# Two expert mixtures whose activations stay in PSUM, rounded by ScalarE and completed by VectorE

## The reference

```python
# mixture one (_L1_ffn_ref): E=8 experts, 128 -> 512 -> 128
h1 = jnp.einsum('bth,efh->btef', x, w1) + b1
h1 = jax.nn.gelu(h1, approximate=False)
expert_outputs = jnp.einsum('btef,ehf->bteh', h1, w2) + b2
# the top 2 of the router's logits, softmax over them, weighted sum
...
# mixture two (_L2_ffn_ref): E=8 experts, 128 -> 2 x 256 -> 128
gu = jnp.einsum('th,eih->tei', x, w13_weight)
gate, up = (gu[..., :INTER], gu[..., INTER:])
act = jax.nn.silu(gate) * up
act = act * combine[:, :, None]
out = jnp.einsum('tei,ehi->th', act, w2_weight)
```

## Time and profile before

| | |
|---|---|
| time, median of three runs | 500.97 us (497.62 to 504.19) |
| span of the profiled execution, first to last instruction | 496.1 us |
| its own time beside the span | not recorded; the median of the runs is 4.9 us above the span |
| PE busy | 412.7 us, 83% |
| DVE busy | 363.1 us, 73% |
| ACT busy | 201.8 us, 41% |
| POOL busy | 197.1 us, 40% |
| mean granted TensorE clock | 0.875 |

### The profile page before, as it was taken

The page is one execution under the profiler, slowest core; times in us unless marked ns, Lnnn a source line. Parts: engine busy times, 40 slices in busy tenths (PEclk is TensorE's granted clock), DMA queues, the critical chain, the costliest instruction groups (busy, mean ns, idle before and its releaser), DMA issues.

```text
span 496.1 us, 5961 instructions
## 1 busy us (share of the span) xinstructions
PE 412.7 (83%) x1982; PEld 315.9 (64%) x1982; DVE 363.1 (73%) x690; ACT 201.8 (41%) x351; POOL 197.1 (40%) x162
## 2 busy tenths in 40 slices
PE   1747888868799999999699997499999986899965
PEld 0526664866566666676379996366666644799834
DVE  4211858577569999998777748959999997777256
ACT  1100131325377666654174531234444321645245
POOL 4100106312568988885110006236576634000052
PEclk9999795675899999999599996679999985999757
DMA  8300000010110011110001000011111000000001
GB/s 272 150 0 0 2 0 1 1 44 0 46 46 18 25 44 42 32 32 2 0 0 33 1 2 0 0 38 32 32 33 32 1 1 0 1 1 0 2 0 42
DMA packets 8638, 12.52 MB, mean 25 GB/s; under 512 B 1131, under 2 KB 4757, under 8 KB 8613
## 3 DMA queue, kind: packets, MB, share of 16 engines
q1 hardware_dynamic: 7984, 11.58, 7.2%
q0 software_dynamic: 96, 0.32, 0.3%
q10 hardware_dynamic: 533, 0.31, 0.2%
HBM read 11.54 MB, written 0.52 MB: 24 GB/s over the span
## 4 chain that ended last, share of the span: by engine, by line
PE 40%; DVE 30%; issue 15%; ACT 7%; POOL 4%; DMA 2%; SPq 0%; DVEq 0%; ACTq 0%; POOLq 0%
DVE rhi L1065 7%; PE bank L1544 6%; PE bank L1208 3%; PE bank L1526 3%; PE bank L1209 3%; PE bank L1210 3%; DVE shared L1154 3%; DVE rhi L1157 2%; DVE wa L1044 2%; DMA mats<-in_mats 2%; ACT shared L776 2%; PE bank L1216 2%; PE bank L1432 2%; PE bank L1435 1%; POOL rstd L363 1%
## 5 line engine op out<-in xcount | busy, mean ns | idle before, releaser
L363 POOL TENSOR_TENSOR rstd<-var,neghalf 128x4 f32<-128x4 f32 x16 | 16.3, 1018 | 156.5 <-DVE var L809 156.5
L432 POOL TENSOR_TENSOR rlo<-shared,rhi 128x512 fp32r<-128x512 f32 x40 | 56.3, 1408 | 45.3 <-DVE rhi L1157 22.7
L1208 PE MATMUL bank<-hhi,wuh 128*128 128x512 f32 x128 | 53.6, 419 | 9.6 <-issue 4.9
L1065 DVE CAST rhi<-shared 128x512 fp32r<-128x512 f32 x48 | 53.4, 1114 | 7.3 <-ACT shared L675 7.3
L675 ACT ACTIVATE shared<-bank,b1s 128x512 f32<-128x512 f32 x64 | 43.9, 687 | 27.3 <-PE bank L1210 25.7
L1209 PE MATMUL bank<-hlo,wuh 128*128 128x512 f32 x128 | 53.1, 415 | 0.0
L1210 PE MATMUL bank<-hhi,wul 128*128 128x512 f32 x128 | 52.7, 411 | 0.0
L1432 PE MATMUL bank<-rhi,wdh 128*128 128x512 f32 x96 | 41.5, 432 | 10.7 <-POOL rlo L432 8.7
L442 POOL TENSOR_TENSOR wb<-wb,wa 128x512 f32<-128x512 f32 x28 | 41.0, 1463 | 14.8 <-DVE wa L1044 14.8
L1124 DVE TENSOR_REDUCE small<-bank 128x6 f32<-128x462 f32 (+1 forms) x48 | 27.8, 579 | 19.2 <-PE bank L1210 19.2
L1071 DVE TENSOR_TENSOR rlo<-shared,rhi 128x512 fp32r<-128x512 f32 x32 | 37.7, 1178 | 5.2 <-ACT rhi L679 4.7
(11 more groups left out here) (272 smaller groups left out, 924.3 us busy)
## 6 DMA issues: line engine op xcount, KB each, us to landing
up_raw<-in_w SPq DMA_DIRECT2D x8, 258.0 KB, 2.7
down_raw<-in_w SPq DMA_DIRECT2D x8, 256.0 KB, 2.9
up_raw<-in_v SPq DMA_DIRECT2D x8, 256.0 KB, 2.7
down_raw<-in_v SPq DMA_DIRECT2D x8, 128.0 KB, 2.7
const<-in_const SPq DMA_DIRECT2D x1, 913.0 KB, 11.7
mats<-in_mats SPq DMA_DIRECT2D x1, 640.0 KB, 10.2
mats<-in_mats SPq DMA_DIRECT2D x1, 576.0 KB, 9.0
x<-in_x SPq DMA_DIRECT2D x2, 256.0 KB, 3.5
```

The source lines that it names most:

```text
L432: nc.gpsimd.tensor_tensor(rlo[n % 4][:, :], ring[n % 4][:, :], rhi[n % 4][:, :].bitcast(F32), ALU.subtract).then_inc(lo, 1)
L1065: V.tensor_copy(rhi[n % 4][:, :], ring[n % 4][:, :]).then_inc(q["hiD"], 1)
L1208: mm(o, lh, rh, start=start, stop=False)
```

## The change

Mixture one: Gelu writes its result into the bank from which it reads. The rounding reads that bank and is done by ScalarE for chunks 0, 2 and 3 of each four, one chunk late (`high1(n-1)` behind Gelu n), and by VectorE for chunk 1. All rests are VectorE's, from the bank. A bank may be overwritten when the rest of its chunk is done, no longer when the Gelu is.

Mixture two: Silu still writes `ring`, but `mul` writes its product into the gate bank. All roundings are ScalarE's (`high2(n-1)` behind Silu n), all rests VectorE's (`low2(n-1)` behind `mul` n). Hidden n makes the up half first, which waits for `mul` n-2, then the gate half, which waits for the rest of chunk n-2.

GpSimd's `low` and its calls go (L432; those hunks and the renamed semaphores are left out below, and so are unchanged lines around the edits).

```diff
@@ -277,11 +277,8 @@
-        LO_POOL1 = {n for n in range(N1) if n % 4 in (0, 2)}
-        HI_ACT1 = {n for n in range(N1) if n % 4 == 1}
-        LO_POOL2 = {1, 5}
-        ALL1, ALL2 = set(range(N1)), set(range(N2))
-        HI_DVE1, LO_DVE1, LO_DVE2 = ALL1 - HI_ACT1, ALL1 - LO_POOL1, ALL2 - LO_POOL2
+        HI_DVE1 = {n for n in range(N1) if n % 4 == 1}
+        HI_ACT1 = set(range(N1)) - HI_DVE1
         BANKS1 = [1, 2, 3, 7]
@@ -489,8 +478,6 @@
                         split_down(i + 1, 0, C2, r)
-                    if n in LO_POOL2:
-                        low(n, r["hi"], N2 * i + n + 1, r["loP"])
                     if n % 2 == 1:
@@ -660,6 +647,13 @@
+            def high1(i, n):
+
+                if n % N1 not in HI_ACT1:
+                    return
+                act.wait_ge(q["gelu"], N1 * i + n + 1)
+                nc.scalar.activation(rhi[n % 4][:, :], bank[BANKS1[n % 4]][:, :], ACT.Copy).then_inc(q["hiA"], 1)
+
             def body1(i, last):
@@ -672,11 +666,10 @@
                     act.wait_ge(q["h"], g + 1)
-                    nc.scalar.activation(ring[n % 4][:, :], bank[BANKS1[n % 4]][:, :], ACT.Gelu,
+                    nc.scalar.activation(bank[BANKS1[n % 4]][:, :], bank[BANKS1[n % 4]][:, :], ACT.Gelu,
                                          bias=b1s[p][:, c:c + 1]).then_inc(q["gelu"], 1)
-                    if n in HI_ACT1:
-                        act.wait_ge(q["gelu"], g + 1)
-                        nc.scalar.activation(rhi[n % 4][:, :], ring[n % 4][:, :], ACT.Copy).then_inc(q["hiA"], 1)
+                    if n > 0 or not i_is(i, 0):
+                        high1(i, n - 1)
                     if i_is(i, 0) and n in (5, 6):
@@ -692,6 +685,7 @@
             body1(PASSES - 1, True)
+            high1(PASSES - 1, N1 - 1)
             output(PASSES - 1, G1 - 1, G1, C1, q["free"], q["add"], q["ys"])
@@ -732,6 +726,11 @@
+            def high2(i, n):
+
+                act.wait_ge(r["mul"], N2 * i + n + 1)
+                nc.scalar.activation(rhi[n % 4][:, :], bank[BANKG[n % 2]][:, :], ACT.Copy).then_inc(r["hi"], 1)
+
             def body2(i, last):
@@ -747,6 +746,8 @@
                     nc.scalar.activation(ring[n % 4][:, :], bank[BANKG[n % 2]][:, :], ACT.Silu).then_inc(r["silu"], 1)
+                    if n > 0 or not i_is(i, 0):
+                        high2(i, n - 1)
                     if n % 2 == 1:
@@ -754,6 +755,7 @@
             body2(PASSES - 1, True)
+            high2(PASSES - 1, N2 - 1)
             output(PASSES - 1, G2 - 1, G2, C2, r["free"], r["add"], r["ys"])
@@ -1060,16 +1062,14 @@
                     g = N1 * i + n
-                    if n not in HI_ACT1:
+                    if n in HI_DVE1:
                         dve.wait_ge(q["gelu"], g + 1)
-                        V.tensor_copy(rhi[n % 4][:, :], ring[n % 4][:, :]).then_inc(q["hiD"], 1)
-                    if n not in LO_POOL1:
-                        if n in HI_ACT1:
-                            dve.wait_ge(q["hiA"], len(HI_ACT1) * i + before(HI_ACT1, n + 1))
-                        else:
-                            dve.wait_ge(q["hiD"], len(HI_DVE1) * i + before(HI_DVE1, n + 1))
-                        V.tensor_tensor(rlo[n % 4][:, :], ring[n % 4][:, :], rhi[n % 4][:, :].bitcast(F32),
-                                        ALU.subtract).then_inc(q["loD"], 1)
+                        V.tensor_copy(rhi[n % 4][:, :], bank[BANKS1[n % 4]][:, :]).then_inc(q["hiD"], 1)
+                        dve.wait_ge(q["hiD"], len(HI_DVE1) * i + before(HI_DVE1, n + 1))
+                    else:
+                        dve.wait_ge(q["hiA"], len(HI_ACT1) * i + before(HI_ACT1, n + 1))
+                    V.tensor_tensor(rlo[n % 4][:, :], bank[BANKS1[n % 4]][:, :], rhi[n % 4][:, :].bitcast(F32),
+                                    ALU.subtract).then_inc(q["lo"], 1)
                     if n % 4 == 2:
@@ -1147,18 +1147,20 @@
+            def low2(i, n):
+
+                dve.wait_ge(r["hi"], N2 * i + n + 1)
+                V.tensor_tensor(rlo[n % 4][:, :], bank[BANKG[n % 2]][:, :], rhi[n % 4][:, :].bitcast(F32),
+                                ALU.subtract).then_inc(r["lo"], 1)
+
             def body2(i, last):
                 for n in range(N2):
                     g = N2 * i + n
                     dve.wait_ge(r["silu"], g + 1)
-                    V.tensor_tensor(ring[n % 4][:, :], ring[n % 4][:, :], bank[BANKU[n % 2]][:, :],
+                    V.tensor_tensor(bank[BANKG[n % 2]][:, :], ring[n % 4][:, :], bank[BANKU[n % 2]][:, :],
                                     ALU.mult).then_inc(r["mul"], 1)
-                    dve.wait_ge(r["mul"], g + 1)
-                    V.tensor_copy(rhi[n % 4][:, :], ring[n % 4][:, :]).then_inc(r["hi"], 1)
-                    if n not in LO_POOL2:
-                        dve.wait_ge(r["hi"], g + 1)
-                        V.tensor_tensor(rlo[n % 4][:, :], ring[n % 4][:, :], rhi[n % 4][:, :].bitcast(F32),
-                                        ALU.subtract).then_inc(r["loD"], 1)
+                    if n > 0 or not i_is(i, 0):
+                        low2(i, n - 1)
                     if n % 2 == 1:
@@ -1166,6 +1168,7 @@
             body2(PASSES - 1, True)
+            low2(PASSES - 1, N2 - 1)
             for j in range(G2 - B, G2):
@@ -1448,7 +1451,7 @@
                     pe.wait_ge(q["ul"], 2 * i + p + 1)
-                wait_positive(pe, q["gelu"], g - 3)
+                wait_positive(pe, q["lo"], g - 3)
                 w = slice(c * P, (c + 1) * P)
@@ -1467,10 +1470,7 @@
                                start=True, stop=True).then_inc(m["b2"], 1)
-                    if n in LO_POOL1:
-                        down(i, n, last, C1, G1, q, q["loP"], len(LO_POOL1) * i + before(LO_POOL1, n + 1))
-                    else:
-                        down(i, n, last, C1, G1, q, q["loD"], len(LO_DVE1) * i + before(LO_DVE1, n + 1))
+                    down(i, n, last, C1, G1, q, q["lo"], N1 * i + n + 1)
@@ -1489,7 +1489,7 @@
             body1(PASSES - 1, True)
-            pe.wait_ge(q["gelu"], N1 * PASSES)
+            pe.wait_ge(q["lo"], N1 * PASSES)
             finish(0, q, G1)
@@ -1595,8 +1595,10 @@
                 wait_positive(pe, r["mul"], g - 1)
-                for bk, off in ((BANKG[n % 2], 0), (BANKU[n % 2], F2)):
+                for bk, off in ((BANKU[n % 2], F2), (BANKG[n % 2], 0)):
                     w = slice(off + c * P, off + (c + 1) * P)
+                    if off == 0:
+                        wait_positive(pe, r["lo"], g - 1)
                     last = mm3(bank[bk][:, :], wuh[p][:, w], wul[p][:, w], hhi[b][:, :], hlo[b][:, :], True, True)
@@ -1608,10 +1610,7 @@
                         weights_T(1, n)
-                    if n in LO_POOL2:
-                        down(i, n, last, C2, G2, r, r["loP"], len(LO_POOL2) * i + before(LO_POOL2, n + 1))
-                    else:
-                        down(i, n, last, C2, G2, r, r["loD"], len(LO_DVE2) * i + before(LO_DVE2, n + 1))
+                    down(i, n, last, C2, G2, r, r["lo"], N2 * i + n + 1)
```

More of the change, by code:

```diff
@@ L240, in flamingo_program @@
         q = {n: sem(f"q_{n}") for n in
-             ["h", "gelu", "hiA", "hiD", "loD", "loP", "free", "uh", "ul", "dh", "dl", "ys", "row", "mult", "add"]}
+             ["h", "gelu", "hiA", "hiD", "lo", "free", "uh", "ul", "dh", "dl", "ys", "row", "mult", "add"]}
         r = {n: sem(f"r_{n}") for n in
-             ["g", "silu", "mul", "hi", "loD", "loP", "free", "uh", "ul", "dh", "dl", "ys", "row", "mult", "add"]}
+             ["g", "silu", "mul", "hi", "lo", "free", "uh", "ul", "dh", "dl", "ys", "row", "mult", "add"]}
         kv = {n: sem(f"kv_{n}") for n in ["pe", "act", "pool", "rep", "reps", "bd", "hi"]}
@@ L427, in _ @@
                 norm(k)
-            def low(n, hi, count, lo):
-                pool.wait_ge(hi, count)
-                nc.gpsimd.tensor_tensor(rlo[n % 4][:, :], ring[n % 4][:, :], rhi[n % 4][:, :].bitcast(F32),
-                                        ALU.subtract).then_inc(lo, 1)
             def add(i, j, groups, mult, done):
@@ L453, in body1 @@
                         split_down(i + 1, 0, C1, q)
-                    if n in LO_POOL1:
-                        low(n, q["hiD"], len(HI_DVE1) * i + before(HI_DVE1, n + 1), q["loP"])
                     if i_is(i, 0) and n == 11:
```

## The result

The changed kernel takes 506.45 us in the median (505.13 to 510.46, four runs) against 502.44 us before, a ratio of 1.0128 with an interval of 1.0074 to 1.0182. So it is slower by some 1.3%: the whole interval lies above 1, and the difference is under 2%. 505.9 us was forecast. Single executions can be over 1.5% slower than the fastest of the same kernel; the ratios leave these out, so a ratio can differ from the quotient of two medians.

A forecast was written before the change was run, and what follows sets the result against it. Mixture one was held by VectorE and GpSimd hindering each other, mixture two would be by a loop of handovers; 496.1 - 9.2 + 14.1 + 4.9 gave 505.9 us, range 498 to 518 us.

The forecast's parts named there:

- Mixture one, TensorE's floor: Four chunks in mixture one take 6.09 us on TensorE; ten waits of 0.74 us for GpSimd's rests go, 7.4 us.
- Its start: Mixture one's first down: ScalarE rounds chunk 0 during VectorE's routing, VectorE ends the rest at 125.3 us; 1.5 us off.
- Its end: Mixture one's last down, at 233.08 us, loses the 0.28 us idle before it; 0.3 us off.
- The cast from PSUM: VectorE's cast of chunk 1 of each four in mixture one, now reading PSUM, takes 0.6 us.
- The slack of 0.3 us: Chunk 3 before a weight copy in mixture one: rest ready after 3.6 us, needed after 3.9, so the wait stays hidden.
- Mixture two's loop: From one chunk's last gate matmul through Silu, product and rest to the next: 2.95 us a chunk against 2.56 before.
- rival three: Granted clock falls to 1.2 GHz in mixture two's idle gaps: 540 us if throughout, 523 us for half; chance 0.12.
- The drain: End of mixture two: 0.2 us shorter, the last rounding no longer queuing behind another Silu.
- The start of mixture two: Silu 2 and 3 stand behind weights on ScalarE; chunk 4's last matmul at 334.9 instead of 331.20 us, 3.7 us lost.
- Rival one: Not slower: mixture two's handovers overlap, its loop below 2.77 us a chunk; 495.5 to about 500 us; chance 0.13.
- rival two: Slower: mixture one's in-place Gelu takes 0.99 us or more, ScalarE's group 6.5 us; 6.4 us more, 512.3 us; chance 0.13.
- The sum: Whole kernel: span 496.1 - 9.2 + 14.1 = 501.0 us, plus 4.9 us between span and median: 505.9 us, 1% slower.

The follow-up runs named there:

- own_keys_splits_later: Changed kernel, mixture two's roundings and rests behind their own chunk, last attention's key products moved into it, GpSimd's first pass awaiting combine weights: 485.60 us, ratio 0.9707.
- two_only: Mixture two as changed, mixture one as in the kernel before: 517.79 us, ratio 1.0307 against the kernel before.
- two_low_own: Changed kernel, but in mixture two VectorE forms the rest of chunk n ahead of the product of n+1; ScalarE's lag stays: 508.83 us, ratio 1.0168.
- two_gate_first: Changed kernel with the halves of mixture two's hidden step in the old order, gate half first: 534.67 us, ratio 1.0621.
- one_ring: Changed kernel, but mixture one's Gelu writes to the SBUF buffer ring, where roundings and rests read it: 508.17 us, ratio 1.0123.

## Why the prediction was right

- **Mixture one, TensorE's floor.** 6.09 us a group were forecast as the new pace, 6.10 came. Ten waits of 0.74 us are gone, 7.4 us.
- **Its start** was forecast at 1.5 us and brought 0.7 (from chunk 3's last hidden matmul to the first down 4.23 us before, 3.56 after). The step that failed was that VectorE is free at 124.6 as before. This trace is 2.1 us ahead of the one before, so that would be 122.5; the first rest started at 123.31. GpSimd, without the rests ahead of it, reached its weights while VectorE was still at the routing, and a small instruction with two SBUF sources stood behind it:

```profile
121.56 1.26 POOL L392 TENSOR_TENSOR wdl<-down_raw,wdh 128x512 fp32r<-128x512 f32 x1 [2.67 <-ACT wdh L549]
...
121.91 1.00 DVE L1012 TENSOR_TENSOR rank<-rank,rinv 128x64 f32<-128x64 f32 x1
...
124.14 0.47 PE L1435 MATMUL bank<-rhi,wdh 128*128 128x512 f32 x1 [2.93 <-DVE rlo L1071]
```

  The same instruction took 0.22 us in the kernel before; own_keys_splits_later put this to the test. Its end brought nothing of the 0.3 us, since the last down still waits for its rest:

```profile
223.05 0.51 PE L1435 MATMUL bank<-rhi,wdh 128*128 128x512 f32 x1 [0.23 <-DVE rlo L1071]
```

  Together 7.9 us instead of 9.2.
- **The cast from PSUM** on VectorE was put at 0.6 us and took 0.681 in the median of 16. VectorE had room for it, so nothing came of it.
- **The slack of 0.3 us** at a group's last chunk held: no wait of TensorE for a rest from 136 to 220 us.
- **Mixture two's loop** was forecast at 2.95 us and measured 2.98; two_only, two_low_own and two_gate_first put its parts to the test (2.98, 2.88 for 2.86, 3.72 for 3.66). From chunk 4 to chunk 31 that makes 0.8 us. A further 0.6 us is one step of 3.59 us (326.31 to 329.90), in which the granted clock had gone to its 1.2 GHz level (0.57 from 326 to 330 us) after two waits of 1.1 and 1.9 us for the rests of chunks 1 and 2; rival three, for one chunk. The drain, from chunk 31's last hidden matmul to the last down, was to be 0.2 us shorter and isn't: 4.34 us before, 4.35 after.
- **The start of mixture two**: chunk 2 to chunk 4 took 10.42 us instead of 6.76, 3.7 us more, as forecast.
- **Rival one** fell, **rival two** too (the Gelu in place got shorter, below). **Rival three** showed for 3.6 us and never in the steady part, not even in two_gate_first from 355 to 435 us, where TensorE was busy 13.7 to 14.9 us of every 20; at the start of that kernel's mixture two it showed for 6 us.
- **The sum** was made with 4.9 us around the span, taken from the median. The changed kernel's profiled execution took 505.88 us with a span of 504.1, so 1.8 us lie around it; the rest was the distance of the profiled execution from the median. Span to span the forecast was +4.9 us, the traces say +8.0, of which 1.3 are the size of mixture one's gain, 1.6 that of mixture two's loss and 0.2 the unchanged stretches. The medians differ by 4.0 us (506.45 and 502.44), half of what the traces say; the four runs of the kernel before alone lie 6.6 us apart. The mechanism of both mixtures was right; that the time was hit to within 1 us is luck, since both mixtures came out slower than forecast by 2.9 us together.

## What to carry to other kernels

Moving work off busy engines pays only where they set the pace. Before a step is put one item later in a queue, look for a buffer that is held until it is done: here a lag of one chunk on two queues and two banks held until the end made a loop of 2.98 us out of work that TensorE does in 2.36, and the same edit without the lag is 2 to 3% faster than the kernel before. An assistant engine can cost more than it brings: taking GpSimd's 32 rests back to a VectorE that looked full (24.83 of 25 us) made mixture one 5.7 us shorter, since beside GpSimd the casts had taken 1.142 us in the median and now take 0.421. And a change of several parts needs an experiment for each: here one line brought most of mixture one's gain.

## What the runs showed of the hardware

Two writes to PSUM and a read that no row of before showed. The Gelu from a bank into the same bank takes 0.662 us in the median against 0.688 into SBUF, 26 ns less. The product into PSUM takes 0.696 us in the median against 0.679 into SBUF in the kernel before, 17 ns more:

```profile
L669 ACT ACTIVATE bank<-bank,b1s x64: 651/662/679, 118.6 to 219.9; 128x512 f32<-128x512 f32 x64
```

```profile
L1160 DVE TENSOR_TENSOR bank<-shared,bank x32: 689/696/697, 312.8 to 408.4; 128x512 f32<-128x512 f32 x32
```

The Gelu goes the way of the Trainium skill ("ScalarE: Activation LUTs", section "Step-by-step: what each stage is for"), which calls ScalarE's writes to PSUM the faster ones. The product goes the way of the page "Perfetto Trace Analysis" of the Trainium skill, section "Optimizing Scalar/DVE Operations", but the 65 ns that one could expect by it, an estimate, were 17; the measurement decides.

The cast of a bank takes VectorE 0.681 us, where the shortest from SBUF took 0.411:

```profile
L1067 DVE CAST rhi<-bank x16: 680/681/683, 123.9 to 218.4; 128x512 fp32r<-128x512 f32 x16
```

Beside GpSimd, VectorE's small instructions with two SBUF sources were held up as much as its large ones. 128x64 elements took 1.00 instead of 0.22 us, 128x128 took 2.35 instead of 0.28 us, each until the GpSimd instruction beside it had ended (122.91 and 122.82 us, 309.79 and 309.65 us). Rests with one source in PSUM stayed at 0.691 us in the mean of 64 and 0.694 at most; with both sources in SBUF the same 64 took 0.918 us in the mean and 1.776 at most (one_ring). The page "SBUF — State Buffer" of the Trainium skill describes it (section "SBUF: two separate sides") as a lock that the first comer holds for its whole instruction; these rows agree.
